# Planner of a one-core transformer layer: weight rounding ranked last, five products under way in the last two units

## The reference, cut to what matters

```python
q, k, v = heads(xn @ Wq.T + bq), heads(xn @ Wk.T + bk), heads(xn @ Wv.T + bv)   # xn = layernorm(x)
q, k = rope(q), rope(k)
att = softmax(where(tril, q @ k.T / 4, -inf))
x = x + (att @ v) @ Wo.T + bo
x = x + fp4_linear(silu(fp4_linear(xn2, w_gate)) * fp4_linear(xn2, w_up), w_down)  # xn2 = layernorm(x)
# fp4_linear rounds both operands to FP4 (blocks of 16 with a common scale) and multiplies
```

## Time and profile before

| | us |
|---|---|
| median of 3 runs | 1295.78 |
| lowest, highest | 1288.91, 1295.86 |
| profiled execution, its own time | 1292.66 |
| its span, first to last instruction | 1290.9 |
| PE busy | 1203.7 |
| DVE busy | 1093.9 |
| ACT busy | 755.4 |
| POOL busy | 476.9 |

### The profile page before, as it was taken

How to read it: one execution, slowest core, us unless ns; L and a number is a source line. 1 busy time by engine, 2 the same in 40 slices (tenths; PEclk the granted TensorE clock), 3 DMA queues, 4 the chain that set the end, 5 groups by cost and what they waited for, 6 DMA issues and landing times.

```text
span 1290.9 us, 40076 instructions
## 1 busy us (share of the span) xinstructions
PE 1203.7 (93%) x16718; PEld 669.9 (52%) x16718; DVE 1093.9 (85%) x2932; ACT 755.4 (59%) x1630; POOL 476.9 (37%) x501
## 2 busy tenths in 40 slices
PE   8679999899999899999999899989999999999967
PEld 7345454454555445545565465545645554545545
DVE  6799998889997998999469799899899999885366
ACT  5246776466565476575655457456656566676621
POOL 3945655544213132122345663311122123014345
PEclk9779999899999999999999999989999999999989
DMA  4735323302101101101044222121111200000000
GB/s 108 183 96 163 103 77 88 99 26 68 43 28 51 51 3 51 35 27 45 10 109 128 81 77 77 51 61 35 38 34 44 59 11 3 19 2 18 5 22 16
DMA packets 79504, 72.40 MB, mean 56 GB/s; under 512 B 25934, under 2 KB 65744, under 8 KB 79312
## 3 DMA queue, kind: packets, MB, share of 16 engines
q1 hardware_dynamic: 76296, 68.76, 19.7%
q10 hardware_dynamic: 3028, 1.09, 0.3%
HBM read 45.07 MB, written 24.35 MB: 54 GB/s over the span
## 4 chain that ended last, share of the span: by engine, by line
PE 60%; DVE 24%; DMA 4%; ACT 4%; issue 3%; POOL 3%; SPq 1%; ACTq 0%; POOLq 0%; DVEq 0%
PE bank L992 13%; PE bank L968 11%; PE bank L1004 10%; PE bank L947 10%; DVE piece_max L1371 8%; DVE bank L1368 7%; PE bank L1123 5%; PE bank L1063 4%; ACT prob L1257 3%; PE bank L1097 2%; PE bank L1071 1%; PE bank L1114 1%; DVE piece_max L1368 1%; DMA q_mem<-max_rows 1%; DMA a_mem<-in_L_attn_x 1%
## 5 line engine op out<-in xcount | busy, mean ns | idle before, releaser
L1257 ACT ACTIVATE prob<-bank 128x512 f32<-128x512 f32 (+3 forms) x1280 | 594.2, 541 | 269.7 <-PE bank L968 152.6
L1371 DVE TENSOR_REDUCE piece_max<-bank 128x1 f32<-128x512 f32 x768 | 487.3, 676 | 9.4 <-PE bank L947 7.9
L968 PE MATMUL bank<-q_mem,k_mem 99*32 99x512 bf16 (+12 forms) x5120 | 388.0, 344 | 15.5 <-DMA q_mem<-max_rows 11.3
L947 PE MATMUL bank<-k_mem,q_mem 96*32 96x512 bf16 (+14 forms) x5120 | 379.5, 346 | 10.3 <-DVE piece_max L1368 5.9
L992 PE MATMUL bank<-prob,V 128*32 128x512 f32 (+3 forms) x2560 | 294.8, 533 | 13.5 <-ACT prob L1257 9.1
L968 PEld LDWEIGHTS bank<-q_mem,k_mem 99*32 99x32 bf16 x5120 | 144.5, 97 | 166.7 <-issue 70.3
L947 PEld LDWEIGHTS bank<-k_mem,q_mem 96*32 96x32 bf16 x5120 | 134.1, 97 | 186.2 <-issue 104.4
L1596 POOL TENSOR_TENSOR c_mem<-c_mem 128x256 f32<-128x256 f32 (+2 forms) x74 | 85.4, 1155 | 380.1 <-DVE c_mem L1470 380.1
L1368 DVE CUSTOM_DVE_ANT_0 bank<-bank,past_keys 128x32 f32<-128x32 f32 (+15 forms) x512 | 208.1, 468 | 3.3 <-PE bank L947 3.2
L992 PEld LDWEIGHTS bank<-prob,V 128*32 128x32 f32 x2560 | 70.4, 110 | 65.8 <-ACT prob L1257 30.5
L973 PE MATMUL bank<-mask_kq,ident_h 128*32 128x64 bf16 (+3 forms) x2048 | 101.6, 201 | 0.0
(11 more groups left out here) (177 smaller groups left out, 1337.9 us busy)
## 6 DMA issues: line engine op xcount, KB each, us to landing
output_dram<-attn SPq DMA_DIRECT2D x28, 256.0 KB, 3.0
parts_dram<-a_mem SPq DMA_DIRECT2D x13, 512.0 KB, 3.8
q_mem<-parts_dram SPq DMA_DIRECT2D x32, 192.0 KB, 3.1
k_mem<-parts_dram SPq DMA_DIRECT2D x32, 192.0 KB, 3.6
q_mem<-parts_dram SPq DMA_DIRECT2D x32, 128.0 KB, 3.1
k_mem<-parts_dram SPq DMA_DIRECT2D x32, 128.0 KB, 3.4
c_mem<-in_L_attn_x SPq DMA_DIRECT2D x30, 128.0 KB, 2.2
out<-c_mem SPq DMA_DIRECT2D x30, 128.0 KB, 1.7
```

What stands on the lines that cost most here:

```text
L947: m = pe.matmul(b[COLUMNS * h:COLUMNS * (h + 1), of], q_rows(u)[0:TERM_ROWS, h, block * COLUMNS:(block + 1) * COLUMNS], k_rows(k0 // CHUNK ...
L968: mm = pe.matmul(b[k0:k0 + COLUMNS, since:CHUNK], k_rows(j // TPC, g)[:, h, first:first + COLUMNS], q_rows(u)[:, h, since:CHUNK], start=Tr ...
L1257: act.activation(prob[:, n % NP, off:CHUNK], bank_of("st", n)[:, off:CHUNK], ACT.Exp, scale=SCALE).then_inc(drained("st", n)[0], 1)
L1371: r = dve.tensor_reduce(most, scores, AX.X, ALU.max)
```

## The change

Two edits in the planner. `w` goes from 0 to -20000: where several jobs could begin at once on an engine, a step of a weight is taken only if it has been ready for more than 20 us longer than the others (less their own leads). And for the score products of units 30 and 31 the exponential five back has to be planned, not three. No instruction and no semaphore is added or removed; all else is what the planner makes of it.

```diff
@@ -46,7 +46,7 @@
 
 HANDOVER_NS = dict(pe=195, act=200, dve=145, pool=150, sp=0, aq=0)
 DMA_TURN_NS, DMA_NS, DMA_KB_PER_NS, DIVIDE_NS, JOIN_NS, BESIDE_NS = 460, 1500, 0.2, 96, 150, 2500
-SOONER_NS = dict(a=0, w=0, xn=10000, s=200, st=0, pv=-1000, place=10000, norm=200, c=(0, -2000), tile=1000)
+SOONER_NS = dict(a=0, w=-20000, xn=10000, s=200, st=0, pv=-1000, place=10000, norm=200, c=(0, -2000), tile=1000)
 
 
 class Waits:
@@ -394,11 +394,12 @@
     def rehearse_probabilities():
         for m, (u, j, off) in enumerate(steps):
             c = units[u][0] % NCHUNKS
+            in_flight = 5 if u >= len(units) - 2 else ST_IN_FLIGHT
             for h in range(GROUP):
                 n = GROUP * m + h
                 room = [("pv", (n - NP) // GROUP)] if n >= NP else []
                 yield from plan.wait([("place", u, 2), ("key ones", c), ("masks",)] + room
-                                     + ([("drain", "st", n - ST_IN_FLIGHT)] if n >= ST_IN_FLIGHT else []))
+                                     + ([("drain", "st", n - in_flight)] if n >= in_flight else []))
                 yield from plan.through(("st", n), 0.43 * (CHUNK - off) + 20 * (j >= c * TPC), "act",
                                         52 + 0.833 * (CHUNK - off), [("place", u, 2)], room, divided=True)
```

## The result

The changed kernel takes 1285.55 us (median of 7 runs, 1279.82 to 1289.55), the kernel before 1295.78 us beside it: a ratio of 0.9925 with a 95% interval of 0.9903 to 0.9947. So it is faster by 0.75%, which is within 1%, where the forecast was 1270, 2.0% faster.

A forecast was written before the change was run, and what follows sets the result against it. PE, busy 93% of the span, was taken to bound the kernel, so only its idle time and low clock could move. Terms summed to -23.6, plus 1 for unseen waits: 1292.7 - 22.6 = 1270.1 us, range 1256 to 1292.

The forecast's parts named there:

- The way into unit 4: Start of unit 4, in 100 to 200 us: PE waits behind eleven pieces of maxima, +3 us, bounds 0 and +5.
- a rival that loses 1 us per weight: Put-off roundings meet later ropes; 14 weights each lose 1 us of DVE, +7: 1277 us; no chance apart from the forecast's 0.58.
- The clock: Four 10 us stretches at or after waits at 248, 725 and 856 us: PE's clock stays up, -5 us, bounds 0 and -7.
- The tail: Behind the last exponential: more tile work covers a 7.0 us wait, last tiles together add 5; -2 us, bounds -7 and +9.
- Start: Ahead of the first score product: no weight transposes stand there, half of a 4.8 us wait goes, -2.4 us, bounds 0 and -4.8.
- 200 to 300: Stretch in us: weight 15's 4.07 us wait is covered by unit 9's products, and one more us goes; -5.1 us.
- 300 to 600: Stretch in us: gates and ups cover a 2.4 us wait for a rounding into unit 12; -2 us, bounds 0 and -3.
- 600 to 900: Stretch in us: tile work fills PE's waits at the starts of units 20 and 24; -8.1 us, bounds 0 and -12.
- Five under way: Last units, 1160 to 1231 us: sooner exponentials only change places with tile work; 0 us, bounds -3.7 and +2.
- Tail at its own pace: Rival: added tail tiles cost 15.0 us each, not 10.7, and half the 600 to 900 term goes; 1283 us, chance 0.20.
- Slower: Rival: DVE's pace sets when units end, so attention ends only 20.6 us sooner, the tail grows by 31.5; 1307 us, chance 0.10.
- More: Rival: the lower clock over 0 to 100 us goes too, half of 14 us; 1263 us, chance 0.12.

The follow-up runs named there:

- the turns moved: Changed kernel with the turns of weights 6 and 7 planned behind unit 4's second score product instead of ahead of its first: 1284.81 us, 0.9911 of before.
- the undoing of the early part: Changed kernel with `w` at -20000 only once eight weight pieces are turned, or in the second sequence, and 0 until then: 1275.75 us, 0.9845 of before.
- the semaphore: Changed kernel with POOL's first rope step of pair 6 made to wait for the end of unit 4's placing chain on DVE: 1286.86 us, 0.9942 of before.
- the reductions: Changed kernel with all small steps of the chain that places the maxima written as TENSOR_REDUCE: 1279.70 us, 0.9881 of before.
- the experiment with filled waiting time: Kernel before the change, with 50 small unread products on PE ahead of weight 15's transposes, where PE sat idle: 1296.01 us, 1.0005 of before.
- the fastest: Changed kernel with `w` at 0 until eight weight pieces are turned, and the placing chain written as TENSOR_REDUCEs: 1269.63 us, 0.9817 of before.

## Why the prediction was wrong

**The way into unit 4, the step that failed.** It stood as "+3 with bounds 0 and +5". The distance from unit 0 to unit 4 grew by 6.1 us in the first profile, and by 8.8 (the change again), 12.8 (`w` only) and 8.7 (the turns moved) in the next three with the early weights put off. The sum counted PE's and DVE's own durations for eleven pieces. It left out what POOL does at that moment: six rope steps of pair 6 back to back, then weight 7's last rounding step. These hold DVE's small steps, and they hold weight 7. With both out of the way the distance is 56.6 us, 2.4 to 4.5 more than with the order of before (54.2 and 52.1): that is within the 0 to +5 that the sum had counted, and what is above it is what it left out. The row for it was there, a CAST of 1.25 us beside a rope step, and I wrote of it as a rival that loses 1 us per weight, in the average; in the repeated kernel it loses 5 us at one place, where everything hangs on it. In the first profile the chain's steps took 1.06 and 0.7 us each, and PE lost 3.3 us behind the rope, at weight 7. That rival, which also said that the roundings that are put off would meet later ropes, was near in kind: the undoing of the early part (0.9845), the semaphore (0.16 us), and the reductions (0.9881) each show it. It was not the rounding's steps that were held, though, but the chain of the maxima.

**The clock, -5, didn't come.** PE's busy time fell by 1.6 us. The falls of the earlier trace rows went, and others came: 0.83 in 200 to 210 and 680 to 690, 0.84 and 0.82 in 980 to 1000 (behind a wait of 2.29 us for a placing DMA), and the largest at 130 to 140, behind the new wait: 0.50 with PE busy 8.75 of 10 us is 4.4 us by my own rule.

```profile
120.00:130.00 10.00, 5.28 (x84) 2.62 (x82) 8.52 (x16) 1.64 (x4) 10.00 (x11) 1.00 0.43 116
130.00:140.00 10.00, 8.75 (x76) 2.97 (x80) 8.64 (x18) 5.69 (x10) 3.14 (x3) 0.50 0.41 110
```

"Without the waits the clock has no cause to fall" held for its four stretches, but the clock fell behind new waits. And the experiment with filled waiting time shows that the term's rule was too dear where DVE sets the pace: 1.2 us of its 2.6 came back at the place, and nothing that can be told in the total. Over a whole kernel busy time and clock go together roughly: from the kernel before (0.974, PE busy 1203.7) to the fastest (0.984, 1192.5), PE is busy 11.2 us less, and 0.010 x 1290.9 is 12.9 us; but at 0.977 one profile has 1203.3 us and another 1199.1. The sentence that puts 7.8 us for the 5 makes a slip besides: the sum would be 1267.3, not 1267.6.

**The tail, -2, was +2.7.** Idle time behind the last exponential is 19.8 us, not 17.1, well inside -7 to +9. The 7.0 went as said, and 4.0 and 4.8 took its place:

```profile
1233.10 1.54 PE L1115 MATMUL bank<-ident,k_mem 128*128 128x128 f32 x6 [3.96 <-POOL k_mem L1603]
...
1264.33 1.51 PE L1115 MATMUL bank<-ident,c_mem 128*128 128x128 f32 x6 [4.77 <-POOL c_mem L1603]
```

The second stands ahead of the last `down` but one (the last turn is at 1270.89 and waits for nothing), with three tiles coming through together: the "+5" of the sum. The first I had not seen.

**What held.** *Start*, -2.4: with TENSOR_TENSORs left in the chain, unit 0's first score product begins at 72.3 to 74.4 us in the seven profiles whose early weights are put off, and at 74.7 to 76.7 in the five others, in the mean 73.2 and 75.8, so -2.6. But as idle time, which the sum counts, it came to nothing: the stretch 0 to 100 shows +1.6, and in the mean it holds 26.1 us of idle time in those seven profiles and 26.5 in the five. The sooner unit 0 won no idle time here. *200 to 300*, -5.1: -5.7. *300 to 600*, -2: -1.9. *600 to 900*, -8.1: -10.0. *Five under way*, 0 (-3.7 to +2): -4.4 alone (0.34% of 1295.8), just outside its bounds though its interval reaches inside them, and not to be told from 0 on top of the first edit.

**The signs.** The last exponential ends at 1190.6, where 1180 to 1190 was said and 1200 was the limit:

```profile
1187.86 2.76 ACT L1258 ACTIVATE prob<-bank 128x384 f32<-128x384 f32 x10
```

There is no wait of 4 us on L1029, L969 waits 6.2 us for the DMA (4 to 6 said), no tail wait of 7 us, and 600 to 900 is at 8.7 us and not 18. PE's idle time is 75.9 us and not 70. The clock is below 1.00 in four stretches between 200 and 1150, where one or two were said. So the mechanism of the middle stands. The forecast had -22.6 and the two profiled executions lie 12.9 apart; the 9.7 between are made up of the start (-2.4 said, +1.6 measured as idle time: 4.0), 100 to 200 (1 said, 2.7 measured: 1.7), the clock (-5 said, -1.6 in PE's busy time: 3.4) and the tail (4.7), less 4.1 for 200 to 1190, where more was won than said, and for the 1 us of waits that no row showed. The rest is in how the medians lie: the two profiled executions are 12.9 us apart and the medians 10.2, since mine was reckoned from a profiled time 3.1 below its median and the new one lies 5.7 below.

**The rivals.** *Tail at its own pace*, 1283, is what the time looks like, by another cause: the 600 to 900 term, of which it took half away, came in full. *Slower* fell with the time. The last exponential did end 39 us sooner (31.5 was its bar), but that bar tells nothing: with `w` alone it ends only 7.4 us sooner, and the time is as good. *More* fell with the clock of the start, 0.86 over 0 to 100 where it was 0.81.

## What to carry to other kernels

Before work is put off, look at what stands on every engine where it would have been done, and on which engine it lands: here the order won its gain in the middle and paid in the first 130 us, and putting off only what is behind the start took 0.9925 to 0.9845. A short step that everything waits for is written in a form that a busy neighbour engine can't hold up; of two waits that lie side by side, taking away one may measure as nothing (0.9911 for the turns moved, 0.9925 and 0.9927 for the change), and only the trace tells that the other stands behind it.

## What the runs showed of the hardware

A DVE step of 0.16 us (CAST, or TENSOR_TENSOR from SBUF) that meets back-to-back TENSOR_TENSORs of POOL may get in between two of them (1.06, 0.71, 0.70, 0.71 us) or be held to the end of the whole run (5.45 us over five steps). Both came up in one kernel, in two executions. Others were held for 4.79 us (TENSOR_TENSOR) and 6.57 us (CAST). The Trainium skill's "SBUF — State Buffer", "Who interferes with whom", says of DVE in a two-port mode beside GpSimd that whoever issues first gets the shared pair of ports for the whole instruction. I read that as a wait for one POOL step, 1.26 us; the rows show more than four in a row, and what decides between the two cases is open. A TENSOR_REDUCE of the same 16 elements took 0.16 to 0.20 us beside the same POOL steps.
